# Layer 0 attention of a two-layer kernel: heads in pairs on 64-row tiles of the array, row maxima over stacked 64-query blocks, keys in half the slots

## What is computed

```python
qkv = jnp.einsum('btd,ed->bte', x, w_in) + b_in        # x is already layer-normed
q, k, v = jnp.split(qkv, 3, axis=-1)                   # each to (B, 16, 512, 8)
scores = jnp.einsum('bhqd,bhkd->bhqk', q, k) * scale
allowed = jnp.abs(idx[:, None] - idx[None, :]) <= 128
scores = jnp.where(allowed[None, None, :, :], scores, -1e30)
attn = jax.nn.softmax(scores, axis=-1)
ctx = jnp.einsum('bhqk,bhkd->bhqd', attn, v)
...
x = x + (xn + attention(xn)) + quantized_ffn(xn)       # layer 0
x = x + attention1(ln(x)) + mixture_of_experts(ln(x))  # layer 1, untouched
```

## Time and profile before

| | us |
|---|---|
| median of 3 runs | 840.89 |
| the runs | 838.93 to 842.55 |
| span of the profiled execution | 837.0 |
| TensorE busy | 643.9 (77%) |
| VectorE busy | 509.8 (61%) |
| GpSimd busy | 424.6 (51%) |
| ScalarE busy | 381.4 (46%) |
| layer 0: first to last score matmul | 52.4 to 493 |

### The profile page before, as it was taken

The page is one execution under the profiler, slowest core; times in us unless marked ns, Lnnn a source line. Parts: engine busy times, 40 slices in busy tenths (PEclk is TensorE's granted clock), DMA queues, the critical chain, the costliest instruction groups (busy, mean ns, idle before and its releaser), DMA issues. The chain is left out here.

```text
span 837.0 us, 17110 instructions
## 1 busy us (share of the span) xinstructions
PE 643.9 (77%) x4397; PEld 370.2 (44%) x4398; DVE 509.8 (61%) x1469; ACT 381.4 (46%) x837; POOL 424.6 (51%) x523
## 2 busy tenths in 40 slices
PE   2346996997969969789699977787875279999950
PEld 0132443544435435344354534565554236666630
DVE  5657775785748747577677716766656524444425
ACT  2202662753735727447357554454433124444420
POOL 6653562752825626438347333666665315555530
PEclk9999998997979989899989997888989669999975
DMA  1222022021121120221211024111110112222219
GB/s 51 90 75 79 27 71 80 20 96 61 52 77 57 65 81 23 87 70 46 93 44 53 14 64 180 41 52 42 44 44 29 55 35 75 75 74 74 72 29 301
DMA packets 53029, 56.44 MB, mean 67 GB/s; under 512 B 6577, under 2 KB 46901, under 8 KB 51136
## 3 DMA queue, kind: packets, MB, share of 16 engines
q1 hardware_dynamic: 44384, 45.01, 16.9%
q0 software_dynamic: 4352, 8.47, 3.0%
q10 hardware_dynamic: 4224, 2.10, 0.8%
HBM read 32.34 MB, written 23.21 MB: 66 GB/s over the span
## 5 line engine op out<-in xcount | busy, mean ns | idle before, releaser
L625 DVE TENSOR_REDUCE mneg<-A 128x1 f32<-128x256 f32 x496 | 223.8, 485 | 121.9 <-PE A L784 115.7
L511 ACT ACTIVATE Pb<-SB 128x512 f32<-128x512 f32 (+1 forms) x256 | 177.6, 702 | 184.4 <-PE SB L806 183.8
L806 PE MATMUL SB<-Qs,Ks 128*128 128x384 bf16 (+1 forms) x512 | 116.8, 313 | 42.4 <-DMA Qs<-mT 34.4
L777 PE MATMUL A<-Ks,Qs 128*128 128x256 bf16 x496 | 136.0, 313 | 17.3 <-DMA Ks<-parts_dram 8.4
L784 PE MATMUL A<-mask,ident 128*128 128x128 bf16 x496 | 125.8, 254 | 2.5 <-issue 2.5
L389 POOL TENSOR_SCALAR_AFFINE_SELECT Pb<-Pb 128x512 f32<-128x512 f32 x96 | 61.2, 638 | 130.8 <-ACT Pb L511 129.9
L1576 POOL DMA_INDIRECT results<-y,xt x72 | 70.7, 983 | 73.1 <-issue 47.0
L816 PE MATMUL PV<-Pb,Va 128*32 128x256 f32 (+1 forms) x1024 | 98.9, 459 | 1.6 <-POOL Pb L394 1.5
L806 PEld LDWEIGHTS SB<-Qs,Ks 128*128 128x128 bf16 x512 | 37.4, 99 | 128.3 <-issue 93.1
L394 POOL TENSOR_SCALAR_AFFINE_SELECT Pb<-Pb 128x512 f32<-128x512 f32 x96 | 61.6, 642 | 49.8 <-ACT Pb L511 49.1
L1138 POOL DMA_INDIRECT expert_rows<-pay,pos x64 | 63.7, 995 | 35.9 <-DVE pay L1324 18.8
(11 more groups left out here) (205 smaller groups left out, 1055.6 us busy)
## 6 DMA issues: line engine op xcount, KB each, us to landing
xt<-expert_rows SPq DMA_DIRECT2D x72, 65.0 KB
yb<-results SPq DMA_DIRECT2D x8, 512.0 KB, 7.5
parts_dram<-qp SPq DMA_DIRECT2D x9, 384.0 KB, 2.5
parts_dram<-kp SPq DMA_DIRECT2D x9, 384.0 KB, 2.5
Qs<-parts_dram SPq DMA_DIRECT2D x16, 192.0 KB
Ks<-parts_dram SPq DMA_DIRECT2D x16, 192.0 KB
xb<-in_x SPq DMA_DIRECT2D x9, 256.0 KB, 2.8
base_dram<-base SPq DMA_DIRECT2D x9, 256.0 KB, 2.1
```

The costliest lines, as they stand in the source:

```text
L511: act.activation(Pb[:, kt, 2 * half:2 * half + 2, 0:w], SB[u % 2][:, :, 0:w], ACT.Exp).then_inc(act_exp, 1)
L625: nc.vector.tensor_reduce(mneg[:, par, qb * HG + h:qb * HG + h + 1], bank_of(step, n, banks)[:, 0:window(qb)[1]], AX.X, ALU.max, negate=Tr ...
L777: nc.tensor.matmul(out[:, 0:w], Qs[pg][:, h // 2, qb * P:(qb + 1) * P], Ks[pg][:, k_slot(h), lo:lo + w], start=True, stop=True)
L806: mm = nc.tensor.matmul(SB[u % 2][:, j, 0:w], Ks[p][:, k_slot(h), kt * P:(kt + 1) * P], Qs[p][:, h // 2, lo:lo + w], start=True, stop=True)
```

## The change

1. `Ks` has 8 slots: even head in partitions 0 to 47, odd head in 64 to 111, as in `Qs`. VectorE's clearing of `Ks` and GpSimd's zero fill of `Qs` go, and so does the copy that cleared the extra rows of `Qs` (two DMAs in each `load_q`).
2. `scores` multiplies rows 0 to 49 and rows 64 to 113 in two matmuls, each on a tile of 64 rows by 128 columns of the array.
3. `piece` handles a pair of heads for one 64-query block: first the mask over all 128 rows (now 64 or 2 x 64 columns, with `start=True`), then two matmuls on tiles of 64 x 64, one for each head, into the lower and the upper partitions of one bank. The key window of a block is 192, 256 or 320 wide (`reach`). A step still has 16 pieces.
4. The 16 columns of maxima are turned in one transpose (32 x 128) in place of four, and the DMA to `Qs` is cut finer (2 x 16 x 64 in place of 2 x 2 x 512).

```diff
+HROW = MROW + 2
+HP = P // 2
+NQ = T // HP
+SUBS = ((0, 2), (1, 3), (7, 4), (6, 5))
...
+def reach(s):
+
+    lo, hi = max(0, HP * s - P), min(T, HP * s + HP + P)
+    return lo, hi - lo
...
-    short, j = k % 2 == 0, k // 2
-    return ((0, NT - 1) if short else (1, NT - 2))[j // HG], j % HG
+    u, second = k // 2, k % 2
+    return SUBS[u // 2][second], u % 2
...
-    Ks = [sb(f"Ks{i}", [P, H, T], BF16) for i in range(2)]
+    Ks = [sb(f"Ks{i}", [P, H // 2, T], BF16) for i in range(2)]
...
-                r0 = 64 * par + MROW
-                sp.dma_start(Qs[pg][r0:r0 + 2, :, :], Qs[pg][r0 + 2:r0 + 4, :, :]).then_inc(dma_stack, 16)
...
-                sp.dma_start(Qs[pg][r0:r0 + 2, 2 * hg:2 * hg + 2, :],
-                             mT[4 * par:4 * par + 4, hg % 2, :]).then_inc(dma_m, 16)
+                sp.dma_start(Qs[pg][r0:r0 + 2, 2 * hg:2 * hg + 2, :].rearrange("r a (s q) -> r (a s) q", q=HP),
+                             mT[:, hg % 2, HP * par:HP * par + HP]).then_inc(dma_m, 16)
...
-        fill_q(0)
+        wait(pool_const, 11)
+        for ks in Ks:
+            pool.memset(ks[:].bitcast(F32), ONE_PAIR).then_inc(pool_fill, 1)
...
-        dve.wait_ge(pool_fill, 2)
-        clear_k(0)
...
-            nc.tensor.matmul(out[:, 0:w], Qs[pg][:, h // 2, qb * P:(qb + 1) * P], Ks[pg][:, k_slot(h), lo:lo + w],
-                             start=True, stop=True)
-
-            if 0 < qb < NT - 1:
-                ends, masks = out[:, 0:4 * P].rearrange("p (n w) -> p n w", w=2 * P)[:, :, 0:P], mask[:]
+            if 1 < s < NQ - 2:
+                ends, masks = out[:, 0:4 * P].rearrange("p (n w) -> p n w", w=2 * P)[:, :, 0:HP], mask[:]
             else:
-                ends, masks = (out[:, w - P:w], mask_hi) if qb == 0 else (out[:, 0:P], mask_lo)
-            mm = nc.tensor.matmul(ends, ident16[:], masks, start=False, stop=True, skip_group_check=True)
+                ends, masks = (out[:, w - HP:w], mask_hi) if s < 2 else (out[:, 0:HP], mask_lo)
+            nc.tensor.matmul(ends, ident16[:], masks, start=True, stop=True, skip_group_check=True)
+            for r0 in (0, HP):
+                mm = nc.tensor.matmul(out[r0:r0 + HP, 0:w], Qs[pg][r0:r0 + MROW, a, HP * s:HP * s + HP],
+                                      Ks[pg][r0:r0 + MROW, a, lo:lo + w], start=False, stop=True,
+                                      skip_group_check=True)
             mm.then_inc(pe_A, 1)
...
-                h = HG * hg + 2 * half + j
-                mm = nc.tensor.matmul(SB[u % 2][:, j, 0:w], Ks[p][:, k_slot(h), kt * P:(kt + 1) * P],
-                                      Qs[p][:, h // 2, lo:lo + w], start=True, stop=True)
+                rows, a = slice(HP * j, HP * j + HROW), 2 * hg + half
+                mm = nc.tensor.matmul(SB[u % 2][:, j, 0:w], Ks[p][rows, a, kt * P:(kt + 1) * P],
+                                      Qs[p][rows, a, lo:lo + w], start=True, stop=True)
```

More of the change, by code:

```diff
@@ L45 @@
 KRUNS = ((0, 3), (3, 2), (5, 1))
-NLOAD = 2 * (len(QRUNS) + len(KRUNS) + 1)
+NLOAD = 2 * (len(QRUNS) + len(KRUNS))
+HROW = MROW + 2
+HP = P // 2
+NQ = T // HP
+SUBS = ((0, 2), (1, 3), (7, 4), (6, 5))
 def window(t):
@@ L70, in ahead @@
     return [(2, u % UNITS)]
-def k_slot(h):
-    return h % 2 * (H // 2) + h // 2
 def layer0(nc, ctx, x, w_inT, b_in, w_outT, b_out, wqT, wscale, fbias, x1_dram, buf, later):
@@ L102, in layer0 @@
     ident16 = sb("ident16", [P, P], BF16)
-    mask = sb("mask", [P, 2, P], BF16)
+    mask = sb("mask", [P, 2, HP], BF16)
     mask_lo, mask_hi = mask[:, 0, :], mask[:, 1, :]
@@ L130, in layer0 @@
     Qs = [sb(f"Qs{i}", [P, H // 2, T], BF16) for i in range(2)]
-    Ks = [sb(f"Ks{i}", [P, H, T], BF16) for i in range(2)]
+    Ks = [sb(f"Ks{i}", [P, H // 2, T], BF16) for i in range(2)]
     Va = [sb(f"Va{i}", [P, NT, H, 32]) for i in range(2)]
-    mneg = sb("mneg", [P, 2, NT * HG])
-    mp = sb("mp", [P, 2, NT, 8], BF16)
-    mT = sb("mT", [8, 2, T], BF16)
+    mneg = sb("mneg", [P, 2, 2 * NQ])
+    mp = sb("mp", [P, 2, 4 * NQ], BF16)
+    mT = sb("mT", [4 * NQ, 2, P], BF16)
     Pb = sb("Pb", [P, NT, HG, 3 * P])
@@ L243, in _ @@
         store_parts(0, 1)
+        load_q(0, 0)
         wait(pool_fill, 1)
-        load_q(0, 0)
-        wait(dve_fill, 2)
         load_k(0, 0)
@@ L254, in _ @@
         sp.dma_start(base_dram[1], base2[:]).then_inc(dma_base_w, 16)
-        wait(pool_fill, 4)
-        wait(dve_fill, 4)
+        wait(pool_fill, 2)
         def body(b, p, first, last):
@@ L315, in _ @@
                                pattern=[[-1, P]], channel_multiplier=1).then_inc(pool_const, 1)
-        pool.affine_select(out=mask_lo, in_=mask_lo, compare_op=ALU.is_ge, fill=NEG, base=0,
-                           pattern=[[1, P]], channel_multiplier=-1).then_inc(pool_const, 1)
-        pool.affine_select(out=mask_hi, in_=mask_hi, compare_op=ALU.is_ge, fill=NEG, base=0,
-                           pattern=[[-1, P]], channel_multiplier=1).then_inc(pool_const, 1)
-        def fill_q(i):
-            pool.memset(Qs[i][:].bitcast(F32), 0.0).then_inc(pool_fill, 1)
-        def fill_k(i):
-            pool.memset(Ks[i][:].bitcast(F32), ONE_PAIR).then_inc(pool_fill, 1)
-        fill_q(0)
+        for half in range(2):
+            wait(pool_const, 7 + 2 * half)
+            rows = slice(HP * half, HP * half + HP)
+            pool.affine_select(out=mask_lo[rows], in_=mask_lo[rows], compare_op=ALU.is_ge, fill=NEG, base=0,
+                               pattern=[[1, HP]], channel_multiplier=-1).then_inc(pool_const, 1)
+            pool.affine_select(out=mask_hi[rows], in_=mask_hi[rows], compare_op=ALU.is_ge, fill=NEG, base=0,
+                               pattern=[[-1, HP]], channel_multiplier=1).then_inc(pool_const, 1)
+        wait(pool_const, 11)
+        for ks in Ks:
+            pool.memset(ks[:].bitcast(F32), ONE_PAIR).then_inc(pool_fill, 1)
         def rstd_of(g):
@@ L399, in _ @@
         base_x(0)
-        fill_k(0)
         quant_scale(0)
@@ L622, in maxima @@
             for n in (2 * u, 2 * u + 1):
-                qb, h = piece_of(n)
+                s, a = piece_of(n)
                 dve.wait_ge(pe_A, 16 * step + n + 1)
-                nc.vector.tensor_reduce(mneg[:, par, qb * HG + h:qb * HG + h + 1],
-                                        bank_of(step, n, banks)[:, 0:window(qb)[1]], AX.X, ALU.max,
+                nc.vector.tensor_reduce(mneg[:, par, a * NQ + s:a * NQ + s + 1],
+                                        bank_of(step, n, banks)[:, 0:reach(s)[1]], AX.X, ALU.max,
                                         negate=True).then_inc(dve_max, 1)
@@ L633, in max_parts @@
                 dve.wait_ge(pe_mT, step - 1)
[L634 to L636 removed]
+            upper, lower = mp[:, par, 0:2 * NQ], mp[:, par, 2 * NQ:4 * NQ]
+            nc.vector.tensor_copy(upper, mneg[:, par, :]).then_inc(dve_mp, 1)
             dve.wait_ge(dve_mp, 2 * step + 1)
[L638 removed]
+            nc.vector.tensor_tensor(lower, mneg[:, par, :], upper, ALU.subtract).then_inc(dve_mp, 1)
         def context(g, qb, bank):
@@ L653, in out_x1 @@
                                     base_r[:].rearrange("p i d -> p (i d)"), ALU.add).then_inc(dve_x1, 1)
-        def clear_k(i):
-            for par in range(2):
-                heads = slice(H // 2, H) if par == 0 else slice(0, H // 2)
-                nc.vector.memset(Ks[i][64 * par:64 * par + 64, heads, :].bitcast(F32), 0.0).then_inc(dve_fill, 1)
         bn(0, range(NT))
@@ L768, in piece @@
         def piece(step, n, hgs, pg, banks=A):
-            qb, h = piece_of(n)
-            h += HG * hgs
-            lo, w = window(qb)
+            s, a = piece_of(n)
+            a += 2 * hgs
+            lo, w = reach(s)
             idx = 16 * step + n
@@ L789, in turn_max @@
             pe.wait_ge(*before)
-            for qb in range(NT):
-                mm = nc.tensor.transpose(misc16[0:8, qb * P:(qb + 1) * P], mp[:, par, qb, :], ident16[:])
-            mm.then_inc(pe_mT, 1)
+            nc.tensor.transpose(misc16[0:4 * NQ, 0:P], mp[:, par, :], ident16[:]).then_inc(pe_mT, 1)
         def scores(b, u, p):
@@ L840, in out_mm @@
             mm.then_inc(pe_out, 1)
-        pe.wait_ge(pool_const, 9)
+        pe.wait_ge(pool_const, 11)
         pe.wait_ge(dma_w, 16 * NCONST)
```

16 lines of the change are left out of this document (4 added, 12 removed).

## The result

The changed kernel takes 963.99 us (median of 4 runs, 961.16 to 993.18), the kernel before in the same comparison 841.72 us (838.93 to 843.00): a ratio of 1.143, 95% interval 1.139 to 1.146. The ratio leaves out the run of 993.18 us, which was in a slower state than the other three. I had forecast 866 us, at most 918. The direction is right, the size is not: the loss is 122 us where 25 stood.

A forecast was written before the change was run, and what follows sets the result against it. TensorE was taken as the bound. Layer 0's net cost +37 us, VectorE waits -12, half clock behind stalls +5, DMAs -3 and start -2 gave +25 on 840.9: 866 us, range 812 to 918.

The forecast's parts named there:

- Where it counts: Layer 0: net loss counts in 200 of 256 slots, +37 us; VectorE waits -12; half clock behind seven stalls +5.
- The clock's rival: Layer 0: clock granted at 1.2 GHz throughout because the array often stands still, TensorE time doubled, 1120 us; chance 0.04.
- The sum for equal clock: Whole kernel: 37 - 12 + 5 - 3 - 2 = +25 us, giving 866 us.
- the 911 us case: Pieces: row tiles writing one bank do not overlap, so pairs run serially, +45 us; chance 0.18.
- The price of a change: TensorE in layer 0: 0.096 us per array shape change, 152 more a batch, 14.6 us a batch.
- Row-only changes: From scores to mask only tile rows change, 32 a batch; counted as costing; if free, 19 us less, 847 us.
- the 787 us case: Layer 0: changing to 64-row tiles costs nothing, so 8.7 us a batch are saved; chance 0.12.
- Weight loads: TensorE pairs: 64-column weight loads taken as hidden, 0 us; if all show, 20 us more, 886 us.
- VectorE: Row maxima: some 440 ns on average as mean width falls from 320 to 272; VectorE waits longer for TensorE.
- Start: Before the first pieces: fills and clearings go, 2 to 4 us earlier, 1 us lost at low clock, -2 us.
- DMAs: Step 1's wait for maxima: dropped copies shorten each of 5 stalls by 0.6 us, -3; stall shorter by about 2.
- by data, a 25th: Copies dropped from the query load: 32 of 800 KB ahead of the maxima, 0.5 us of some 13 us.

The follow-up runs named there:

- e4: Changed kernel plus 20 dense 512-column matmuls, results unread, at each batch's first slot (fifth in the first batch): 870.33 us, 1.037 of the kernel before.
- e7: Kernel before plus the same filler of 20 dense 512-column matmuls a batch, as control: 1.005 of the kernel before, 2.8 us more.
- e1: Kernel before with only the scores moved to 64-row tiles, pieces left on 128 x 128: 0.998 of the kernel before.
- e11: Changed kernel with mask and scores also on 64 x 64 tiles, and query and key loads issued as one DMA per 8 rows: 757.75 us, 0.941 of before.
- e3: Changed kernel with mask and scores also on 64 x 64 tiles, so no shape change within a slot before its values: 0.972 of the kernel before.
- e10: The kernel with mask, pieces and scores all on 64 x 64 tiles, timed again on another chip: 782.54 us, 0.973 of the kernel before.

## Why the prediction was wrong

- **The step that failed is "Where it counts"**: that behind each stall the clock is 0.50 for about 5 us, seven times, +5 us. It was read off the kernel before and carried over to a kernel whose TensorE works otherwise. In its place stand three stretches of 78 to 85 us and half clock from the start to 157.2 us, +89 us by e4 against e7.
- **The clock's rival was drawn wrong.** It was all of layer 0 at 1.2 GHz or nothing, at 1120 us, and got 0.04 because the clock had stayed up through holes of 0.1 us and waits of 0.8. The changed kernel agrees with that argument: from 157 to 210 us the clock is 1.00 through five holes a slot. The question I did not ask was whether it would rise again, once one of the stalls of the earlier trace rows had brought it down. Staying up and coming back up are two questions, and the second needs its own row. The rival also took TensorE's time at half clock as double; it is 1.56 times, since the changes do not stretch with the clock.
- **The sum for equal clock was right in size, in part by luck**: +25 forecast for all, +27 measured in layer 0 (e4 against e7), but three terms were off and nearly cancel, as the next points show. What it assumed: the overlap of row tiles in one bank holds (starts 3 ns apart), so the 911 us case falls. The Trainium skill (TensorEngine Tiling (Array Packing), Gotcha 1: PSUM Pressure) says that different row tiles cannot access one bank at the same time; here they write different partitions of one bank and do, so the measurement decides.
- **The price of a change** was put at 0.096 us; it is 0.10 to 0.13, 0.114 on the mean of the five. Row-only changes, which I had left open, cost 0.11 (e1). By the Trainium skill (same page, Key Properties) changing the mode drains TensorE, and the trace agrees at every change seen; it gives no price. 64-row tiles change no cheaper than 32-column ones, so the 787 us case falls too. 0.018 us more on 152 changes in 6.25 batches would be +17 us. What takes them back are the waits, before with the filler (e7) and the changed kernel with it (e4):

```profile
PEld A L777 <- DVE mneg L625: 37.3, 110, 1.3
PEld misc L791 <- DVE mp L638: 10.1, 15, 2.5
PE SB L809 <- DMA Qs<-mT: 12.6, 4, 3.3
```

```profile
PEld A L768 <- DVE mneg L623: 15.7, 76, 0.4
PEld misc L778 <- DVE mp L635: 1.4, 1, 1.4
PE SB L798 <- DMA Qs<-mT: 4.3, 4, 1.3
```

TensorE waits 30 us less for VectorE, where I let 12 go, and 8 less for the maxima's DMA, where the sum has 3. What is left of the difference I did not take apart.
- **Weight loads** do not show, as taken: the holes are 0.10 and 0.11 us before a 64-row pair and 0.11 and 0.12 before the mask.
- **VectorE**: the maxima average 441 ns, as forecast (some 440), and it waits 231 us for TensorE where it waited 116, as forecast.
- **Start**: the first pair begins at 50.1 us, 2.3 earlier than 52.44, in the 2 to 4 us forecast. The first scores come 1.7 us later than before (65.6 for 63.9), with the clock at half throughout.
- **DMAs**: the third batch's stall was 5.3 us in place of 6.70; 1.4 less of forecast 2. But "by data, a 25th" counted bytes, and what sets the landing is the busiest engine (e11).

What stays open: which quantity the gate reacts to, how much of the half-clock start belongs to the change, and why two profiles of one kernel, e3 and e10, differ in the clock at the start (first rise at 96.0 and at 54.1 us).

## What to carry to other kernels

Count changes of the array's tile shape as instructions of 0.11 us each (as measured here), and give all matmuls of an inner loop one shape, even if it takes more of them: here four narrow scores and two narrow masks beat two and one wide ones by 15%. Where a change thins out TensorE's work, ask of each stall in the trace before whether the work behind it would raise the clock again, and print two stretches of equal length at 1.00 and at 0.50. Where a small DMA is late behind large ones, count the rows on each DMA engine before its place in the queue is moved.

## What the runs showed of the hardware that I had not expected

- The granted clock stayed at 0.50 (1.2 GHz) for 78.5, 78.5 and 85.3 us, inside the second of them with TensorE called busy in 53.00 of 53.00 us, in a slot order that keeps 1.00 from 157.2 to 218.7 us once it has it.
- A change of tile shape costs 0.11 us at 2.4 GHz and 0.12 at 1.2 GHz.
- Two 64-row tiles write different partitions of one bank at the same time, starts 3 ns apart.
- An 8-row DMA of 8 KB rows takes SP 0.41 us to issue (4.87 for twelve), one of 24, 16 or 8 rows 0.76 on the mean (4.58 for six).
